# A scan's head means in two fp32r passes, and one buffer for two kinds of FFN evictions

## The reference

```
def step(carry, x):
    Z1 = xk @ W1_s + b1_s
    grad = _ln_fused_l2_bwd(Z1, xv - xk, ln_w, ln_b)
    ...
    Z1_bar = xq @ W1_s - eta_mb * Attn1 @ grad + b1_bar
    W1_new = W1_s - (last_eta * xk).swapaxes(-1, -2) @ grad
    ...
    out = xq + _ln(Z1_bar, ln_w, ln_b)
```

## Time and profile before

| | |
|---|---|
| median of 3 runs | 2029.44 us (2029.36 to 2030.3) |
| profiled execution, its own time | 2030.64 us |
| its span, first to last instruction | 2029.0 us |
| mean granted clock of TensorE | 0.981 |
| busy: TensorE, VectorE, ScalarE, GpSimd | 1883.2, 1205.5, 979.3, 1031.5 us |
| chain that ended last, largest share | TensorE 35% |

### The profile page before, as it was taken

How to read it: one execution, slowest core, us unless ns; L and a number is a source line. 1 busy time by engine, 2 the same in 40 slices (tenths; PEclk the granted TensorE clock), 3 DMA queues, 4 the chain that set the end, 5 groups by cost and what they waited for, 6 DMA issues and landing times. The chain is left out here.

```text
span 2029.0 us, 34753 instructions
## 1 busy us (share of the span) xinstructions
PE 1883.2 (93%) x12632; PEld 1423.4 (70%) x12632; DVE 1205.5 (59%) x2400; ACT 979.3 (48%) x2105; POOL 1031.5 (51%) x904
## 2 busy tenths in 40 slices
PE   5897998898999899889899989999999999999998
PEld 3675777665666665577787867777777777777776
DVE  4662565777786774357335446666666666666663
ACT  3333555555665555544434426444444444444442
POOL 5444566556566654430134337555555555555552
PEclk9898999999999999979999999999999999999999
DMA  7786657436333533141678871232233223322321
GB/s 244 275 298 204 211 157 254 126 108 208 118 116 119 205 112 100 56 142 58 222 244 279 263 263 43 94 115 94 91 128 115 92 79 120 118 78 78 111 100 41
DMA packets 157112, 297.97 MB, mean 147 GB/s; under 512 B 20240, under 2 KB 97296, under 8 KB 150288
## 3 DMA queue, kind: packets, MB, share of 16 engines
q1 hardware_dynamic: 155856, 294.70, 43.0%
q10 hardware_dynamic: 1088, 1.05, 0.2%
HBM read 221.52 MB, written 74.19 MB: 146 GB/s over the span
## 5 line engine op out<-in xcount | busy, mean ns | idle before, releaser
L1968 POOL TENSOR_SCALAR probs<-probs,rsum 128x512 f32<-128x512 f32 x256 | 396.5, 1568 | 245.3 <-DVE rsum L2104 245.3
L2068 ACT ACTIVATE p_tok<-bank 128x512 fp32r<-128x512 f32 x256 | 154.9, 608 | 343.4 <-PE bank L2008 343.3
L2100 DVE TENSOR_REDUCE nmax<-bank 128x1 f32<-128x512 f32 x256 | 158.9, 683 | 93.9 <-PE bank L2000 93.9
L2110 DVE TENSOR_TENSOR p_tok<-bank,p_tok 128x512 fp32r<-128x512 f32 x256 | 173.3, 680 | 15.9 <-ACT p_tok L2068 15.8
L2060 ACT ACTIVATE probs<-bank,nmax 128x512 f32<-128x512 f32 x256 | 173.0, 693 | 2.2 <-DVE nmax L2100 2.2
L60 PE MATMUL bank<-xs,ffn_w 128*128 128x512 f32 x352 | 153.1, 435 | 11.8 <-issue 8.5
L1456 POOL TENSOR_TENSOR y_pieces<-y_tok,y_pieces 128x512 fp32r<-128x512 f32 x48 | 65.8, 1385 | 183.7 <-ACT y_pieces L1661 183.5
L2008 PE MATMUL bank<-ident,probs 128*128 128x128 f32 x1024 | 156.1, 276 | 2.8 <-DVE p_tok L2110 2.8
L2008 PEld LDWEIGHTS bank<-ident,probs 128*128 128x128 f32 x1024 | 121.9, 140 | 50.8 <-issue 27.2
L1090 DVE SCALAR_TENSOR_TENSOR pt<-bank,t_mask 128x256 f32<-128x256 f32 x256 | 91.7, 413 | 97.7 <-PE bank L877 96.3
L61 PE MATMUL bank<-xs,ffn_w 128*128 128x512 f32 x352 | 139.0, 395 | 0.0
(11 more groups left out here) (276 smaller groups left out, 4955.2 us busy)
## 6 DMA issues: line engine op xcount, KB each, us to landing
ffn_w<-ffn_pieces SPq DMA_DIRECT2D x120, 512.0 KB, 3.6
uvo<-uvo_pieces SPq DMA_DIRECT2D x15, 2048.0 KB, 8.7
wq<-wq_pieces SPq DMA_DIRECT2D x16, 1536.0 KB, 6.4
ffn_pieces<-stage SPq DMA_DIRECT2D x30, 512.0 KB, 4.3
xs<-xn_pieces SPq DMA_DIRECT2D x4, 2048.0 KB, 7.8
y_tok<-in_gup SPq DMA_DIRECT2D x32, 256.0 KB, 3.6
wk<-wk_pieces SPq DMA_DIRECT2D x16, 512.0 KB, 3.6
ffn_w<-ffn_pieces SPq DMA_DIRECT2D x16, 384.0 KB, 3.5
```

The lines of the kernel that those rows point to most:

```text
L1968: nc.gpsimd.tensor_scalar(probs[:, u % 8, :], probs[:, u % 8, :], rsum[:, u % 8:u % 8 + 1], None, ALU.mult).then_inc(norm_done, 1)
L2068: nc.scalar.activation(p_tok[:, Q % 2, 0, :, hh * P:(hh + 1) * P], banks[4 + u % 2][:].rearrange("p (k q) -> p k q", k=NBLK), ACT.Copy).th ...
L2100: nc.vector.tensor_reduce(nmax[:, u % 8:u % 8 + 1], banks[u % HG][:], axis=X_AXIS, op=ALU.max, negate=True).then_inc(max_done, 1)
L2110: nc.vector.tensor_tensor(p_tok[:, Q % 2, 1, :, q], banks[4 + u % 2][:].rearrange("p (k q) -> p k q", k=NBLK), p_tok[:, Q % 2, 0, :, q].bi ...
```

## The change

The squares of a closed group are no longer given to TensorE in fp32. ScalarE copies `o_sq` to a high half in fp32r right behind the square, for which it waits for its own square; VectorE subtracts to the low half between the first and the second part's `pt` of the closing step; TensorE takes the means in two fp32r passes in the same place as before, with `avg16` now fp32r, and waits for both halves. The next group's square waits for the low half as well. Down evictions go to the buffer of the up evictions; an up waits for the accumulations of all downs before it, a down for the products of all ups before it.

```
-        bd16, t_mask, avg16 = [s0(n, [P, P]) for n in ("bd16", "t_mask", "avg16")]
+        bd16, t_mask = [s0(n, [P, P]) for n in ("bd16", "t_mask")]
+        avg16 = s0("avg16", [P, P], F32R)
...
-            silu_g, up_sb, hid, dn_sb = [s(n, [P, 2, TB]) for n in ("silu_g", "up_sb", "hid", "down_sb")]
+            silu_g, up_sb, hid = [s(n, [P, 2, TB]) for n in ("silu_g", "up_down_sb", "hid")]
+            dn_sb = up_sb
...
+            osq_hi, osq_lo = s("o_sq_hi", [P, TB], F32R), s("o_sq_lo", [P, TB], F32R)
...
+            ups_before = lambda j: sum(kind_of(i) == "up" for i in range(j))
+            downs_before = lambda j: sum(kind_of(i) == "down" for i in range(j))
...
                     def variances(G):
-                        pe.wait_ge(osq_done, G + 1)
+                        pe.wait_ge(osqhi_done, G + 1)
+                        pe.wait_ge(osqlo_done, G + 1)
                         pe.wait_ge(pt_done, min(NF * (4 * G + 5) + 1, NF * NPART))
-                        nc.tensor.matmul(psp[0][:], avg16[:], o_sq[:], start=True, stop=True).then_inc(ovar_ready, 1)
+                        nc.tensor.matmul(psp[0][:], avg16[:], osq_hi[:], start=True, stop=False)
+                        nc.tensor.matmul(psp[0][:], avg16[:], osq_lo[:], start=False, stop=True).then_inc(ovar_ready, 1)
...
                             elif kind == "up":
                                 if x >= 2:
                                     act.wait_ge(prod_done, x - 1)
+                                if downs_before(j):
+                                    act.wait_ge(acc_done, downs_before(j))
...
                                 if x >= 2:
                                     act.wait_ge(acc_done, x - 1)
+                                act.wait_ge(prod_done, ups_before(j))
...
                             if G >= 1:
                                 act.wait_ge(ovar_ready, G)
+                            if G >= 1:
+                                act.wait_ge(osqlo_done, G)
                             nc.scalar.activation(o_sq[:], obank[:], ACT.Square).then_inc(osq_done, 1)
+                            act.wait_ge(osq_done, G + 1)
+                            nc.scalar.activation(osq_hi[:], o_sq[:], ACT.Copy).then_inc(osqhi_done, 1)
...
                         if ps:
                             factors(ps[0], (2, 3))
+                        G = closes_at(n)
+                        if G is not None:
+                            dve.wait_ge(osqhi_done, G + 1)
+                            if G >= 1:
+                                dve.wait_ge(ovar_ready, G)
+                            nc.vector.tensor_tensor(osq_lo[:], o_sq[:], osq_hi[:].bitcast(F32), ALU.subtract).then_inc(osqlo_done, 1)
```

More of the change, by code:

```diff
@@ L597, in build @@
             wx_zero = sem("ttt_wx_zero")
+            osqhi_done, osqlo_done = sem("ttt_osqhi_done"), sem("ttt_osqlo_done")
             cst_in = [sem("ttt_cst_in0"), sem("ttt_cst_in1")]
```

## The result

The changed kernel took 2036.28 us (median of 10 runs) against 2029.35 us for the kernel before: ratio 1.0028, 95% interval 1.0018 to 1.0038. A second series, with other runs of both, gave 2035.2 against 2030.61 us: ratio 1.0014, interval 1.0005 to 1.0024. By these ratios it is slower by some 3 to 6 us, where I had forecast 2029.8 and a range to 2032.4.

What follows compares the result with a forecast made beforehand. Bound: VectorE's small operations from z to state update, TensorE's queue from there to next z, then a ring of waits. Terms -1.2 + 0.8 + 0.84 = +0.4 us on 2029.44 gave 2029.8 us, range 2026.6 to 2032.4.

Steps and rivals of the forecast that it cites:

- One buffer: First up after four downs, near 748 us, waits for GpSimd's accumulation and delays step 31's state update: +0.84 us.
- The means on TensorE: Two fp32r passes save 0.40 us per group, counting in few state-carrying steps: together -1.2 us, bounds 0 and -1.6.
- three steps: Steps 12, 22 and 28, where TensorE or ScalarE fed by it ends last before the state update: 0.40 us each.
- Step 22: ScalarE's `sg_bd` ends at 593.37, TensorE gets there only at 594.15, so 0.40 us is won.
- The halves: High-half copy delays ScalarE's queue 0.69 us, covered at steps 11 to 29; VectorE's 0.68 us low half costs nothing.
- The delays of `o_std` after the last state: Steps 32 to 42: ScalarE's 0.69 us partly reaches `o_std`; together +0.8 us, bounds -2.0 and +1.4.
- Step 32: `o_std` shows no wait behind the table load, so all but some 0.2 us of ScalarE's delay arrives: +0.5.
- Step 42: Table load already ended last; VectorE's low half comes about 0.4 us later than the means started: 0.
- TensorE as the bound: Rival: all 16 x 0.40 us is won, -6.4, with +0.84, giving 2023.9 us; chance 0.06.
- VectorE blocking `pt`: Rival: the subtraction blocks `pt` in 16 closing steps, 0.3 us each, median 2034.6 us; chance 0.07.
- The hidden copy: Rival: ScalarE's 0.69 us does not reach `o_std`, tail gives -2.0, sum -2.4, 2027.1 us; chance 0.18.
- The lock: Rival: subtraction lengthens GpSimd's operation 0.35 us in steps 32, 34, 36, 40; +1.4, median 2031.3 us; chance 0.13.

Runs made afterwards that it cites:

- the ring: Changed kernel with up and down evictions sharing a ring of three slots, low half written over the square; ratio 0.9995 against the kernel before.
- the isolated edits: Kernel before plus the shared buffer and its waits: ratio 1.0017; kernel before plus only the ups' wait for accumulations of earlier downs: 1.0015.
- three_slots: Changed kernel with a three-slot ring for up and down evictions, low half written over the square; ratio 0.9995 against the kernel before.
- late_high: Changed kernel with the three-slot ring, and ScalarE's high-half copy moved behind the FFN evictions from step 31 on; ratio 1.0004 against the kernel before.
- after: The changed kernel, first series, against the kernel before: 2036.28 us, ratio 1.0028.
- after_again: The same changed kernel timed and profiled again: 2035.2 us, ratio 1.0014 against the kernel before.
- two_of_three: Changed kernel with tiles placed as for the three-slot ring, third slot unused, waits unchanged; ratio 1.0033 against the kernel before, from six executions.
- three_fill: Changed kernel with the three-slot ring and step 31's three later FFN trips moved ahead of its state update; 2030.01 us, ratio 0.9999.

## Why the prediction was wrong

**The step that failed is "One buffer": +0.84, with bounds of 0 and +1.4.** The place, the cause and the engine that passes the delay on were right; of eleven first ups it was this one. Its price was not, and it was taken for the whole price. From z to state update it took 1.35 us more (10.63 to 11.98). Two parts make nearly all of that: the product started 5.66 us after z instead of 4.71, which is 0.95 (forecast 0.84), and it then lasted 1.79 instead of 1.43, which is 0.36. At its new time it ran beside two operations of VectorE on 256 columns, one of which took 0.83 instead of 0.43; at its old time it ran beside a reduction and operations on 16 columns. I had carried the product over at its old duration, though the earlier trace rows held both a pair of 1.78 and one of 1.43. The 1.35 by itself still lies inside the bound of +1.4.

**Nothing stood in the sum for TensorE's clock.** This is what took the result past the range. I noted that the granted clock was within 2% of full and drew from it that "no more is in it". That was a mean over 561 us, and it hides falls to half. I counted the 1.3 us of added idle as time and not as something that the clock answers to, though the trace of before had the answer. After 300 us its scan has three idles of TensorE of over 3 us, 4.33 us until 316.99, 3.98 until 662.10 and 3.86 until 853.68, and the clock fell at each of them, while it stayed behind the 2.47 us at step 31 (columns as in the earlier trace rows):

```profile
853.68 0.50 PE L60 MATMUL bank<-hid_hi,ffn_w 128*128 128x512 f32 x1 [3.86 <-POOL hid_lo L744]
...
314.00:318.00 4.00, 1.01 (x2) 0.83 (x3) 0.00 (x0) 2.14 (x4) 2.20 (x4) 0.62 0.96 407
662.00:666.00 4.00, 3.90 (x11) 3.13 (x12) 1.32 (x4) 0.69 (x1) 1.46 (x3) 0.64 0.95 392
854.00:858.00 4.00, 4.00 (x25) 2.55 (x24) 0.00 (x0) 1.77 (x3) 2.31 (x3) 0.57 0.03 8
```

At step 31 the fall costs 1.2 to 1.7 us more from the state update to `o_std` of step 32 (9.08 to 9.67 against 7.92 with the ring), and 1.6 with the fp32 means (9.22 and 9.26 against 7.66). Wait and clock together, up to `o_std` 40, are +2.5 to +3.0 where I had 0.84 (98.27 to 98.80 against 95.77), and the isolated edits give +3.0, with ratios whose centres are 3.0 and 3.4 us. With this in the sum the forecast would have been 2031.5 to 2032.0 (2029.8 - 0.84 + 2.5 to 3.0), and the range, moved by as much, would have reached 2034.1 to 2034.6. The medians of the changed kernel, 2036.28 and 2035.2, lie above that too; this account does not explain the rest (see what stays open).

**The means on TensorE: -1.2 by three steps.** Measured by z of step 12 to z of step 31: 338.49 before and 337.65 after, -0.84. Over all profiles the six with fp32 means average 339.11 and the eight with two passes 338.44, -0.67; single ones scatter by 1.1 us, because in nine of them the clock fell once behind an idle of 1.7 to 1.8 us near 535 or 607 us. By step: z to z is 0.43 shorter from step 12 to 13, 0.41 from 28 to 29, as forecast with their mechanism. Steps 20 and 24 won 0.1 to 0.2 each, which I had at nothing, and the steps behind the two winners gave back some: step 13 took 18.52 to 18.60 us instead of 18.40 to 18.43, step 29 18.29 to 18.49 instead of 18.16 to 18.17. Why is not shown. In step 12 the two `sg_bd` copies and the update:

```profile
415.22 0.77 DVE L1143 COPY sg_bd<-sg 32x256 f32<-32x256 f32 x2
415.57 0.85 ACT L1059 ACTIVATE sg_bd<-sg 32x256 f32<-32x256 f32 x2
...
416.52 0.65 PE L855 MATMUL bank<-sg_bd,ktz 128*32 128x64 f32 x32 [1.18 <-DVE sg_bd L1143]
```

The update comes 9.45 us after z (407.07), before 9.88. Step 22 won nothing (9.42 against 9.45). I had looked at the end of TensorE's queue and not at the waits inside. In it a matmul waits, with a bank that ScalarE has emptied only just before, in both kernels; first before, then after:

```profile
589.66 0.47 PE L60 MATMUL bank<-xs,ffn_w 128*128 128x512 f32 x1 [0.54 <-issue]
...
589.57 0.47 PE L60 MATMUL bank<-xs,ffn_w 128*128 128x512 f32 x1 [0.96 <-issue]
```

It starts 4.96 us after z in both, and the pause ahead of it grew by 0.42: TensorE came to it earlier and waited the more.

**The halves.** High half 0.63 (forecast 0.63): right. Low half 0.69 (0.68) in ten of the sixteen closing steps, but 1.15 to 1.55 in six, where it meets GpSimd's addition to `q_t`; below the 1.76 that I had allowed for, so VectorE stayed hidden behind `pt`, which waited 0.6 us or more for TensorE in all fifteen closing steps of the changed kernel that have one. The means waited for the halves only in step 42: right. The delays of `o_std` after the last state: step 34 +0.20 (forecast +0.20), 36 +0.24 (+0.20), 38 -0.41 (-0.40), 40 +0.30 (+0.32). Step 32 gave +0.26 by three_slots (7.92 against 7.66) where I had +0.5. There the next operation had started 0.62 us behind the square before the change, not 0.48, so the copy delays it by 0.54 and not 0.69; 0.36 of that reaches the table load, and `o_std` had 0.1 to spare. Step 42 cost up to 0.5 where I had 0 (9.04 against 8.50, though one profile of before has 9.02).

**The rivals.** TensorE as the bound (2023.9) was refuted by the steps (-0.67 from step 12 to 31, where ten times 0.40 would be -4.0), VectorE blocking `pt` by the wait for TensorE that stays (1.49 in step 39, 0.6 at the least). The hidden copy was refuted by 76.84 to 77.17-77.22. The lock did not act where I put it, in the steps behind the last state; where late_high moved the work into its way, it did, and it did in five closing steps before, at no cost. The Trainium skill's rule (SBUF — State Buffer, "SBUF: two separate sides") that I had weighed for the new subtraction acted also on an old operation that the wait had moved. The trace agrees in direction: 1.43 became 1.79.

**What stays open.** From z of step 12 to the last addition the three profiles of before took 461.5, 463.9 and 463.9 us, after, after_again and two_of_three 465.0, 466.3 and 466.1: +2.7 us, or 0.13%. That is as much as the second ratio, 1.0014. The other series of the same waits gave 1.0028 and 1.0033, 3 to 4 us more. Part of it shows ahead of step 12, in code that the change leaves alone: z of step 0 came at 202.3 to 202.7 us in those three, at 199.2 to 200.3 in the three of before, and of this 1.5 us were left at z of step 12. With them GpSimd's last addition starts 4.2 us later (868.2, 869.1 and 869.5 before; 872.0, 873.5 and 873.9), or 0.2%, which lies between the two ratios. three_fill had z of step 0 at 202.1 too and was not slow. I have no cause for it, and one profile for a kernel can't give one.

## What to carry to other kernels

A wait that binds once can cost a whole kernel more than an operation added 16 times (here 3.0 us against 0.6 in the scan's end): list the places where a new wait would have bound in the old trace, follow the one that does to the engine that sets the pace, and price every operation between at its new neighbours, not at its old duration. Add to that the idle which it makes on TensorE: where idle grows from 2.5 to nearly 4 us ahead of work that sets the end, look in the same trace for what the granted clock did after idles of that length. If a buffer must be given up, a ring over both users can lose the wait; here it had three slots, and the low half was written over the square to make room for the third.

## What the runs showed of the hardware

TensorE's granted clock fell to half in 5 of 5 profiles at an idle of 3.8 us at step 31, in 1 of 6 behind 2.4 to 2.5 us, in 0 of 3 behind under 0.9 us, and in 42 of 42 cases at the idles of 3.8 to 4.4 us elsewhere in the scan; behind two idles of 1.7 to 1.8 us it fell in 9 of 28. It can fall before the idle ends, by up to 2.6 us here. The fall at step 31 took 1.2 to 1.7 us more in the work behind it. A GpSimd pair of multiplications took 1.43 us beside a reduction and small operations of VectorE and 1.60 to 1.86 beside operations of VectorE with two inputs and 256 or 512 columns. VectorE's subtraction of 512 columns took 0.69 us alone and 0.80 to 1.55 beside GpSimd. Where it started while an addition of GpSimd ran, it ended 0.55 us after that addition, which kept its 1.26 to 1.29 us.
